# A twelve-layer decoder on one core: semaphores cleared beside the next stage, a shorter start, the output stored in four parts

## What is computed

```python
x = x + retention(layernorm(x))            # l0a
x = x + cross_attention(layernorm(x), ctx) # l0x
x = x + attention_and_experts(layernorm(x))# l0g, then l0f
x = x + linear_layers(layernorm(x))        # l1a
x = x + cross_attention(layernorm(x), ctx) # l1x
x = x + moe(layernorm(x))                  # l1f
x = x + attention_over_sequences(layernorm(x)) # l2a
x = x + cross_attention(layernorm(x), ctx) # l2x
x = x + moe(layernorm(x))                  # l2f
x = x + delta_rule_layers(layernorm(x))    # l3a
x = x + single_head_cross_attention(layernorm(x), ctx) # l3x
x = x + soft_slots_ffn(layernorm(x))       # l3f
```

## Time and profile before

| | us |
|---|---|
| median of 3 runs (2321.5 to 2323.09) | 2321.7 |
| the profiled execution, its own time | 2321.48 |
| its span, first to last instruction | 2319.7 |
| TensorE busy, share of the span | 85% |
| VectorE, ScalarE, GpSimd busy | 46%, 35%, 15% |
| mean granted TensorE clock | 0.897 of full |

### The profile page before, as it was taken

One profiled execution on the slowest core, in us unless ns is written; L12 is line 12 of the kernel. 1 busy time (PEld: TensorE's weight loads), 2 busy tenths in 40 slices (PEclk: granted clock), 3 DMA queues, 4 the chain that ended last, 5 costly groups with the idle time before them and its releaser, 6 DMA issues. The chain is left out here.

```text
span 2319.7 us, 42346 instructions
## 1 busy us (share of the span) xinstructions
PE 1964.8 (85%) x17156; PEld 1355.4 (58%) x17156; DVE 1073.2 (46%) x2487; ACT 822.1 (35%) x1451; POOL 339.4 (15%) x572
## 2 busy tenths in 40 slices
PE   6869469799899986899997868999966786776998
PEld 4637146466567754677774546777755355444776
DVE  4456545433455555621117656211134845755432
ACT  1236135222222224543430045434333142224664
POOL 2242332100000004200000042000010511411000
PEclk8859589899999996999999969999986896987999
DMA  1051311000000015100000141000000000000000
GB/s 59 1 111 51 78 42 29 29 14 14 20 22 22 22 34 111 38 10 19 19 10 6 27 108 34 10 19 19 19 33 3 0 1 3 0 15 1 1 1 19
DMA packets 44322, 62.32 MB, mean 27 GB/s; under 512 B 4481, under 2 KB 38017, under 8 KB 43777
## 3 DMA queue, kind: packets, MB, share of 16 engines
q1 hardware_dynamic: 42402, 58.04, 9.8%
q10 hardware_dynamic: 1728, 1.57, 0.3%
HBM read 25.00 MB, written 1.05 MB: 11 GB/s over the span
## 5 line engine op out<-in xcount | busy, mean ns | idle before, releaser
L1899 ACT ACTIVATE l2f_a<-l2f_bank,l2f_expert 128x512 f32<-128x512 f32 x144 | 98.8, 687 | 137.2 <-PE l2f_bank L1835 137.2
L1846 PEld LDWEIGHTS l2f_bank<-l2f_expert,l2f_a 128*128 128x128 f32 x1152 | 134.1, 192 | 16.7 <-issue 16.5
L1846 PE MATMUL l2f_bank<-l2f_expert,l2f_a 128*128 128x128 f32 x1152 | 134.3, 275 | 0.0
L2024 DVE SCALAR_TENSOR_TENSOR X<-l2f_bank,l2f_W,X 128x128 f32<-128x128 f32 x144 | 40.5, 344 | 200.2 <-PE l2f_bank L1846 200.2
L1835 PE MATMUL l2f_bank<-l2f_xT,l2f_expert 128*128 128x512 f32 x288 | 131.7, 600 | 0.0
L1899 ACT ACTIVATE l1f_a<-l1f_bank,l1f_expert 128x512 f32<-128x512 f32 x128 | 87.8, 687 | 120.1 <-PE l1f_bank L1835 120.1
L1846 PEld LDWEIGHTS l1f_bank<-l1f_expert,l1f_a 128*128 128x128 f32 x1024 | 119.2, 192 | 14.8 <-issue 14.6
L2024 DVE SCALAR_TENSOR_TENSOR X<-l1f_bank,l1f_W,X 128x128 f32<-128x128 f32 x128 | 36.0, 344 | 181.0 <-PE l1f_bank L1846 180.9
L1846 PE MATMUL l1f_bank<-l1f_expert,l1f_a 128*128 128x128 f32 x1024 | 119.3, 275 | 0.0
L1835 PE MATMUL l1f_bank<-l1f_xT,l1f_expert 128*128 128x512 f32 x256 | 117.1, 601 | 0.0
L1454 DVE TENSOR_TENSOR l1a_kv<-l1a_bank,l1a_layer 128x512 f32<-128x512 f32 x96 | 61.9, 686 | 87.0 <-PE l1a_bank L1384 86.8
(11 more groups left out here) (605 smaller groups left out, 4160.2 us busy)
## 6 DMA issues: line engine op xcount, KB each, us to landing
l2f_expert<-in_experts_l2f SPq DMA_DIRECT2D x9, 514.0 KB, 3.6
l1a_layer<-in_layers_l1a SPq DMA_DIRECT2D x12, 385.0 KB, 3.0
l1f_expert<-in_experts_l1f SPq DMA_DIRECT2D x8, 514.0 KB, 3.5
l0x_k_stack<-l0x_k_parts SPq DMA_DIRECT2D x24, 128.0 KB, 3.3
l0g_k_stack<-l0g_k_parts SPq DMA_DIRECT2D x24, 128.0 KB, 2.5
l0f_expert<-in_experts_l0f SPq DMA_DIRECT2D x4, 768.0 KB, 4.2
l1x_k_stack<-l1x_k_parts SPq DMA_DIRECT2D x24, 128.0 KB, 3.2
l2x_k_stack<-l2x_k_parts SPq DMA_DIRECT2D x24, 128.0 KB, 3.2
```

What stands on the lines that cost most here:

```text
L1846: ins = pe.matmul(self.banks[4 + par][:, i * D:(i + 1) * D], self.a[:, par, c, i * T:(i + 1) * T], w2[:, c, :], start=(c == 0), stop=(c == ...
L1899: act.activation(self.a[:, par, c, :], self.banks[c][:, :], ACT.Gelu, bias=self.buf[e % 2][:, 2 * FF + c:2 * FF + c + 1]).then_inc(q["gate ...
L2024: ins = dve.scalar_tensor_tensor(out=x, in0=self.banks[4 + u % 2][:, i * D:(i + 1) * D], scalar=self.W[:, g * GI + i, e:e + 1], in1=x, op0 ...
```

## The change

Semaphores are now handed out from a list of their own for each stage (`signals`) and are given back one stage later. `clear_semaphores` and its blocks are gone. In their place SyncE clears the semaphores of stage n, all of them, at the end of its own list of stage n + 1 (`clear_stale`); those of the last stage are cleared by GpSimd in the closing block. In the first block SyncE no longer waits for the loads; VectorE waits in `l0a`, for the first four sequences ahead of its first statistics and for the rest ahead of the second. In `l3f` SyncE stores four sequences at a time, when they have been added, and waits for the four stores at the end of that stage.

```diff
-BASE_LOADS = 48
+BASE_LOADS = 32
+    def clear_stale(self, eng):
+        for sem in self.stale:
+            eng.sem_clear(sem)
...
     def sem(self, name):
-        s = self.ctx.enter_context(self.k.nc.semaphore(f"{self.tag}_{name}"))
+        s = self.signals.enter_context(self.k.nc.semaphore(f"{self.tag}_{name}"))
...
         @block.sync
         def _(sp):
             k.load(sp, n + 1)
+            k.clear_stale(sp)
...
+            dve.wait_ge(k.first_loaded, 16)
             norms[0].on_vector_stats(dve, 0, rows_of(0))
+            dve.wait_ge(k.base_loaded, BASE_LOADS)
             norms[1].on_vector_stats(dve, 0, rows_of(1))
...
+            k.clear_stale(sp)
+            for g in range(NG):
+                sp.wait_ge(q["added"], (g + 1) * GI)
+                sp.dma_start(k.dram["out"][:, rows(g), :], X[:, rows(g), :]).then_inc(q["stored"], 16)
+            sp.wait_ge(q["stored"], 16 * NG)
...
+        finished = ExitStack()
         for n, name in enumerate(UNITS):
+            signals = ExitStack()
             with ExitStack() as mem:
-                s = Scope(k, mem, name)
+                s = Scope(k, mem, signals, name)
                 if n == 0:
                     open_program(k)
                 BUILD[name](k, s, n)
-                nums = s.sems
-                clear_semaphores(nc, nums)
+            finished.close()
+            finished, k.stale = signals, s.sems
         close_program(k, out)
+        finished.close()
...
-            sp.dma_start(k.X[:, 0:GI, :], k.dram["x"][:, 0:GI, :]).then_inc(k.base_loaded, 16)
+            sp.dma_start(k.X[:, 0:GI, :], k.dram["x"][:, 0:GI, :]).then_inc(k.first_loaded, 16)
...
-            sp.wait_ge(k.base_loaded, BASE_LOADS)
+            if UNITS[0] != "l0a":
+                sp.wait_ge(k.first_loaded, 16)
+                sp.wait_ge(k.base_loaded, BASE_LOADS)
...
-            sp.dma_start(out[:, :, :], k.X[:, :, :]).then_inc(stored, 16)
-            sp.wait_ge(stored, 16)
+            if UNITS[-1] != "l3f":
+                sp.dma_start(out[:, :, :], k.X[:, :, :]).then_inc(stored, 16)
+                sp.wait_ge(stored, 16)
+
+        @block.gpsimd
+        def _(pool):
+            k.clear_stale(pool)
```

More of the change, by code:

```diff
@@ L48, in __init__ @@
         self.base_loaded = ctx.enter_context(nc.semaphore("base_loaded"))
+        self.first_loaded = ctx.enter_context(nc.semaphore("first_loaded"))
         self.ident_loaded = ctx.enter_context(nc.semaphore("ident_loaded"))
@@ L51, in __init__ @@
         self.loads = [0, 0]
+        self.stale = []
         self.tick = ctx.enter_context(nc.semaphore("tick"))
@@ L142, with __init__ @@
 class Scope:
-    def __init__(self, k, ctx, tag):
-        self.k, self.ctx, self.tag, self.sems = k, ctx, tag, []
+    def __init__(self, k, ctx, signals, tag):
+        self.k, self.ctx, self.signals, self.tag, self.sems = k, ctx, signals, tag, []
     def sb(self, name, shape, dt=F32):
@@ L659, in sync @@
         self.k.load(sp, n + 1)
+        self.k.clear_stale(sp)
 class Own(Attention):
@@ L3024, in sublayer_l3_ffn @@
         "se_squared se_rooted se_safed se_inverted se_scaled se_turned se_ready squared rooted safed inverted rooted_d scaled rows_turned "
-        "xT_ready logits maxed expd inverses dnormed turned cT_ready dm_ready slots_made slT_ready up gelud down pr_ready mixed added").split()}
+        "xT_ready logits maxed expd inverses dnormed turned cT_ready dm_ready slots_made slT_ready up gelud down pr_ready mixed added stored").split()}
     steps = range(-2, NB + 1)
@@ L3351, in decoder_kernel @@
     with ExitStack() as ctx:
-        k = Shared(nc, ctx, dram)
+        k = Shared(nc, ctx, {**dram, "out": out})
         k.selectors = Selectors(nc, ctx)
+        finished = ExitStack()
         for n, name in enumerate(UNITS):
+            signals = ExitStack()
             with ExitStack() as mem:
-                s = Scope(k, mem, name)
+                s = Scope(k, mem, signals, name)
                 if n == 0:
@@ L3388, in _ @@
             pool.memset(k.plus[:, :], 0.5)
[L3391 to L3417, removed]
 def close_program(k, out):
```

## The result

The changed kernel took 2306.1 us in the median of 4 runs (2305.0 to 2307.4), the kernel before 2322.4 in the same series. The ratio is 0.9929, with an interval of 0.9917 to 0.9941: 16.3 us less, where 19.35 had been forecast; 2302.3 was the forecast time and 2298 to 2308 its range. The profiled execution took 2305.28, its span is 2303.5.

What follows compares the result with a forecast made beforehand. Each of 13 stages cut apart by barriers has its own bound (TensorE busy 85% of the span); time is their sum plus gaps, start and end. Terms -18.15 - 2.0 + 0.8 = -19.35 gave 2302.3 us, range 2298 to 2308.

Steps and rivals of the forecast that it cites:

- Between the stages: At the 12 clearing blocks, the idle windows from release to release are saved whole: -18.15 us, low bound some 17.
- The clears beside the stages: SyncE's clears, up to 4.9 us in `l3x`, are hidden by its wait at the same stage's end: cost nothing.
- The start: In `l0a`, statistics no longer all wait for `iota`, so TensorE begins at 13.8, not 15.83: -2.0 us, bounds 0 to 2.3.
- Both steps: In `l0a`: first statistics between 5.3 and 6.7 us, second from 11.15, after VectorE waits for `iota`.
- The end: Behind the last addition: 2.3 us store of 256 KB, then 3.9 us of GpSimd clears; 7.0 against 6.2, +0.8 us.
- The sum: Whole kernel: -18.15 - 2.0 + 0.8 = -19.35 us, 2302.3 on the median of the runs.
- The three terms: Between the stages -18.15 us, at the start -2.0, at the end +0.8.
- its own last sentence: Wrong if stage starts show empty gaps over 1 us, half-clock stretches grow, or stage lengths move more than among equals.
- The range: Whole kernel, 2298 to 2308 us, from the bounds of the terms and 3 us of clock scatter; likeliest case 73%.
- The clock rival: TensorE's half clock at stage starts may shift: 9 us at most either way, some 3 scattered; common gain 7%, loss 5%.
- Late code: At 12 stage starts, first instruction fetched from memory after release, at least 1.8 us each: 2323.9, no change; chance 3%.

Runs made afterwards that it cites:

- the medians of the second: The changed kernel run again, unaltered, on another chip beside three further kernels: 2302.7 us against 2323.35 of the kernel before, ratio 0.9919.
- `old_start`: The changed kernel with SyncE's wait for all the first loads put back into the first block: 2307.3 us, ratio 0.9930 to the kernel before.
- `blocks_only`: The kernel before with only the clearing blocks between the stages taken out; old start, single store, last clears on five engines: 2306.5 us, ratio 0.9929.
- `after`: The profiled execution of the changed kernel in its first series, nothing further changed: 2305.28 us.

## Why the prediction was right, and where it was off

- **Between the stages: -18.15 forecast, -18.4 measured** from the last instruction of a stage to the first of the next. The whole window from release to release is gone, and the entry into a stage costs 0.02 us less at each place than the entry behind a clearing block did. In the eight traces without the blocks the 12 gaps are the same 3.8 us. (Of VectorE's 13 waits in the earlier trace rows the one at the first block is 6.6 us; only the 12 others are 1.6 to 2.6.)
- **The clears beside the stages: nothing, as forecast.** The cover in `l3x` went from 32.9 to 27.8 us; four times the clears cost no time that the runs could tell.
- **The start: -2.0 forecast, -2.6 in the profiled pair**, outside the bounds of 0 to 2.3. Both steps went as told. `iota` was there for VectorE at 10.6 in place of 11.1, which is most of the difference. With the new start TensorE began between 12.9 and 13.5 in five traces, with the old between 15.8 and 16.8 in three. So the gain varies by about as much as it was mis-sized.
- **The end: +0.8 forecast, +1.0 measured.** The store took 2.2 us (2.3 forecast). GpSimd's clears took 4.2 us, 0.076 each, not 0.07. The estimate of 2.6 us for this size by the fit of the Trainium skill ("DMA: Bandwidth & Descriptors", section "Anatomy of one DMA") was 0.4 above the trace. Over the profiles the last 256 KB took 2.2 to 3.1.
- **The sum: -19.35 forecast, -16.3 in the first series and -20.7 in the medians of the second** (its ratio gives -18.8). All 9 runs of the changed kernel have a mean of 2304.6, the 28 of the kernel before one of 2322.8: -18.2. The three terms, as the profiled pair has them, make -20.1. The 1.9 us between are inside the stages; with standard errors of 0.9 and 0.3 us of the two means they can't be told from nothing. In the first pair it was 3.9.
- **What the sum took for fixed and wasn't.** The stages were put at their old lengths within 1 us each. In the pair `l0a` grew by 3.2, `l0g` by 1.5 and `l1x` by 1.3, and `l3a` and `l3f` shrank by 1.5 and 1.9. `l0a` differs by more than that between two executions of one program (4.5), but `l1x` and `l3f` don't (0.1 and 0.4 at most). By its own last sentence this part of the prediction failed. The time that the terms were subtracted from was also low: the three runs of 2321.5 to 2323.1 hid a scatter of 2318.8 to 2326.2, and their median lay 1.1 us under the mean of all 28.
- **The range**, 2298 to 2308, doesn't follow from its own bounds: they and 3 us of scatter give some 2298.5 to 2310.1. That 2306.1 lies in it is owed to the 3 us put in for the clock. The measured terms alone, with nothing for the clock, make 2301.6.
- **The clock rival** came in part. The scatter of 3 us that it was given is real: two executions of one program differ by 4.7 us in their stages (2279.4 and 2274.7). Its common loss came in `l0f` to `l2f`, with 2.8 us in the changed kernel and up to 7.2 in others without the blocks, and its gain in `l3f`, with 1.4 to 2.6. They cancel in part: over all stages the means with and without the blocks differ by 0.6 us.
- **Late code** didn't come: the first instruction of a stage stands 0.3 us behind the last of the one before, drain, barrier and jump included. Of the stall at a taken branch that the Trainium skill ("Runtime: NRT & Kernel Launch", section "Instruction fetch mechanics") warns of, these traces show nothing.

What stays open: why the first half-clock stretch of `l0a` begins at 14.8 us in one execution and at 16.6 in the next of the same program, and whether the idle time between the stages by itself moves the stretches in `l0f` to `l2f`. No experiment here moved them at will.

## What to carry to other kernels

Bookkeeping between stages that are cut by barriers is paid in full, by the slowest engine's rate, and can be sized before by windows from release to release; given to an engine that stands idle through the next stage, it costs nothing that these runs could tell. But "the stages didn't change" is to be checked stage by stage: a sum that stays the same can hide a loss in one and a gain in another. At the end of a program there is no next stage: there the same list belongs beside the last store and on several engines. And terms of a few us in a program of 2300 are best measured in the trace, gap by gap, since the medians of 11 and 15 runs couldn't tell 0 from 2.6 us here.

## What the runs showed of the hardware

- One clear of a semaphore takes a sequencer 0.12 us on TensorE, 0.07 to 0.08 on GpSimd and 0.06 on SyncE.
- The last store of 256 KB took 2.2 us in six traces and 3.1 in one (`old_start`), the one of 1024 KB 3.9 in two and 5.4 in one (`blocks_only`).
- A stretch at half clock can begin while TensorE is at work: busy for 9.1 of the 10.2 us ahead of the fall at 74.2 in `after`, and for all of the 10.2 us behind it, at 0.50.
- The same 9472 matmuls of `l0f` to `l2f` kept TensorE busy for 1184.2 to 1192.3 us, by how the half-clock stretches fell, and without the clearing blocks never for less than 1188.0.
